# Linear attention of a four-part network: the last head's work in an order of its own, its gate in another PSUM pair

## What is computed

```python
q = silu(causal_dwconv(x @ Wq)); k = silu(causal_dwconv(x @ Wk)); v = x @ Wv
q, k = layernorm(q), layernorm(k)                  # by head
beta = sigmoid(x @ Wb + bb); gate = silu(x @ Wg)
S = (1 - b) * S + b * outer(v_t, k_t)              # by token and head
o_t = S @ q_t
out = (o * gate) @ Wo
```

## Time and profile before

| What | Value |
|---|---|
| Median of 3 runs | 1116.66 us (1115.64 to 1118.02) |
| Profiled execution: own time | 1122.7 us |
| Its span, first to last instruction | 1121.0 us |
| Busy share: TensorE, VectorE, ScalarE, GpSimd | 93%, 70%, 60%, 45% |
| Mean granted TensorE clock | 0.964 of full |
| First gate SiLU and last gating product, start | 480.9 and 821.5 us |
| First ScalarE instruction of the next block | 822.99 us |

### The profile page before, as it was taken

The page is one execution under the profiler, slowest core; times in us unless marked ns, Lnnn a source line. Parts: engine busy times, 40 slices in busy tenths (PEclk is TensorE's granted clock), DMA queues, the critical chain, the costliest instruction groups (busy, mean ns, idle before and its releaser), DMA issues. The chain is left out here.

```text
span 1121.0 us, 18624 instructions
## 1 busy us (share of the span) xinstructions
PE 1043.5 (93%) x6437; PEld 823.9 (74%) x6437; DVE 782.7 (70%) x1785; ACT 677.7 (60%) x1239; POOL 505.4 (45%) x459
## 2 busy tenths in 40 slices
PE   7999999988998998699999999999889999999997
PEld 5433333337786987588998899889779878888997
DVE  5788888717666655699999999998557546333843
ACT  4478778756643454687887787878545444333454
POOL 3251320113039552377676767767604200446534
PEclk9999999969998998699999999999889999999999
DMA  3434333105224300342311221230010122655200
GB/s 90 85 63 62 65 53 56 49 12 169 76 72 136 56 1 6 113 137 65 101 62 52 86 91 52 62 95 25 20 35 12 48 53 59 182 142 169 76 20 20
DMA packets 80633, 79.28 MB, mean 71 GB/s; under 512 B 29320, under 2 KB 67676, under 8 KB 80540
## 3 DMA queue, kind: packets, MB, share of 16 engines
q1 hardware_dynamic: 80228, 77.66, 25.8%
q10 hardware_dynamic: 312, 0.43, 0.3%
HBM read 65.51 MB, written 1.28 MB: 60 GB/s over the span
## 5 line engine op out<-in xcount | busy, mean ns | idle before, releaser
L705 DVE TENSOR_REDUCE attn_row_max<-attn_rows_q 128x1 f32<-128x512 f32 x256 | 159.1, 682 | 29.4 <-PE attn_rows_q L482 29.2
L617 ACT ACTIVATE attn_probs<-attn_rows_k 128x512 f32<-128x512 f32 x256 | 135.4, 600 | 44.0 <-PE attn_rows_k L496 43.7
L496 PE MATMUL attn_rows_k<-attn_q_stack,attn_k_stack 50*128 50x512 f32 x256 | 96.5, 469 | 14.9 <-ACT attn_probs L617 14.8
L482 PE MATMUL attn_rows_q<-attn_k_stack,attn_q_stack 48*128 48x512 f32 x256 | 97.5, 466 | 1.9 <-DMA attn_q_stack<-attn_part 1.2
L2773 DVE TENSOR_TENSOR late_mids<-late_mids,late_bank 128x512 f32<-128x512 f32 (+1 forms) x50 | 34.3, 687 | 78.5 <-PE late_bank L67 75.5
L482 PEld LDWEIGHTS attn_rows_q<-attn_k_stack,attn_q_stack 48*128 48x128 f32 x256 | 42.1, 186 | 55.5 <-DVE attn_row_max L705 43.7
L65 PE MATMUL late_bank<-net_x_part_low,late_w_T 128*128 128x512 f32 (+1 forms) x192 | 77.9, 406 | 0.0
L66 PE MATMUL late_bank<-net_x_part_low,late_w_T 128*128 128x512 f32 (+1 forms) x192 | 76.1, 396 | 0.0
L67 PE MATMUL late_bank<-net_x_part_low,late_w_T 128*128 128x512 f32 (+1 forms) x192 | 76.0, 396 | 0.0
L510 PE MATMUL attn_ctx<-attn_probs,attn_v 128*32 128x512 f32 x512 | 73.7, 652 | 0.0
L496 PEld LDWEIGHTS attn_rows_k<-attn_q_stack,attn_k_stack 50*128 50x128 f32 x256 | 42.2, 191 | 41.9 <-ACT attn_probs L617 36.1
(11 more groups left out here) (407 smaller groups left out, 3415.5 us busy)
## 6 DMA issues: line engine op xcount, KB each, us to landing
lin_mix<-decay_sums SPq DMA_DIRECT2D x16, 512.0 KB, 4.0
lin_q_dec<-decay_sums SPq DMA_DIRECT2D x16, 512.0 KB, 5.4
gold_weight<-gold_weights SPq DMA_DIRECT2D x16, 256.0 KB, 3.5
attn_k_stack<-attn_part SPq DMA_DIRECT2D x30, 128.0 KB, 3.5
s_raw_ring<-in_L_ffn_Wg SPq DMA_DIRECT2D x12, 256.0 KB, 3.1
s_raw_ring<-in_L_ffn_Wu SPq DMA_DIRECT2D x12, 256.0 KB, 3.9
attn_q_stack<-attn_part SPq DMA_DIRECT2D x32, 64.0 KB, 2.3
gold_raw_w_down<-in_L_ffn_Wd SPq DMA_DIRECT2D x1, 2048.0 KB, 12.9
```

Source lines behind the costliest of these rows:

```text
L482: pe.matmul(ps_q[n % 3][:, :], q_stack[rows, h % SLOTS, r * P:(r + 1) * P], k_stack[rows, h % SLOTS, half * HALF:(half + 1) * HALF], start ...
L496: pe.matmul(ps_k[n % 3][:, :], k_stack[rows, h % SLOTS, t * P:(t + 1) * P], q_stack[rows, h % SLOTS, :], start=True, stop=True).then_inc(s ...
L617: act.activation(probs[:, kk % PB, side * HALF:(side + 1) * HALF], ps_k[n % 3][:, :], ACT.Exp)\
L705: dve.tensor_reduce(row_max[:, tile, half:half + 1], ps_q[n % 3][:, :], axis=AX, op=ALU.max)\
```

## The change

Only the last two steps have an order of their own, on four engines. TensorE's loop ends with step 16. Then come, for head 15: turned keys, keys and values, scores, gate, outputs. The gate of head 15 is projected into bank pair 3 instead of pair 0, once the queries are copied out (`q_T_done`); so keys and values no longer wait for its SiLU but for the states of head 14, which read pair 0. ScalarE splits the last gate's weights ahead of the exponentials of head 15. VectorE makes the states of head 15 ahead of its probabilities. GpSimd decays the values of head 15 ahead of its key rows.

```diff
--- before.py
+++ after.py
@@ -1744,8 +1744,8 @@
             if h + 1 < LH:
                 pe.wait_ge(self.v_copied, h + 2)
             else:
-                pe.wait_ge(self.states_done, h)
-            project("gate", pair[0], self.g_projected)
+                pe.wait_ge(self.q_T_done, LH)
+            project("gate", pair[0] if h + 1 < LH else pair[3], self.g_projected)
 
         def project_v(j):
             p, half = divmod(j, 2)
@@ -1774,7 +1774,10 @@
             i.then_inc(self.scored, 1)
 
         def key_values(h):
-            pe.wait_ge(self.g_acted, h + 1)
+            if h + 1 < LH:
+                pe.wait_ge(self.g_acted, h + 1)
+            else:
+                pe.wait_ge(self.states_done, h)
             pe.wait_ge(self.k_rows_done, h + 1)
             pe.wait_ge(self.v_dec_done, h + 1)
             for c in range(NT - 1):
@@ -1806,7 +1809,7 @@
         rows_k(0)
         project_q(1)
         turn_q(0)
-        for n in self.STEPS[2:]:
+        for n in self.STEPS[2:LH + 1]:
             if live(n - 1):
                 rows_q(n - 1)
             turn_k(n - 2)
@@ -1822,6 +1825,11 @@
             if live(n - 1):
                 turn_q(n - 1)
             outputs(n - 2)
+        turn_k(LH - 1)
+        key_values(LH - 1)
+        score(LH - 1)
+        project_gate(LH - 1)
+        outputs(LH - 1)
 
     def high(self, act, m, src, done):
         act.activation(self.parts[m][0][:, :, :], src[:, :, :], ACT.Copy).then_inc(done, 1)
@@ -1886,7 +1894,7 @@
 
         def silu_gate(h):
             act.wait_ge(self.g_projected, h + 1)
-            act.activation(self.gated_out[:, h, :], self.pair[0][:, :], ACT.Silu).then_inc(self.g_acted, 1)
+            act.activation(self.gated_out[:, h, :], self.pair[0 if h + 1 < LH else 3][:, :], ACT.Silu).then_inc(self.g_acted, 1)
 
         def exp_mix(h):
             act.wait_ge(self.masked, h + 1)
@@ -1946,7 +1954,7 @@
         q_transposed(0)
         silu(1, 1, self.k_conved, self.k_acted)
         exp_mix(0)
-        for n in self.STEPS[2:]:
+        for n in self.STEPS[2:LH]:
             if live(n):
                 high_q(n)
             k_transposed(n - 2)
@@ -1972,6 +1980,14 @@
             if live(n):
                 silu(n, 1, self.k_conved, self.k_acted)
                 copy_v(n)
+        k_transposed(LH - 2)
+        silu_gate(LH - 2)
+        high_gate(LH - 1)
+        exp_mix(LH - 1)
+        norm_k(LH - 1)
+        q_transposed(LH - 1)
+        k_transposed(LH - 1)
+        silu_gate(LH - 1)
 
     def dve_first(self, dve):
         dve.wait_ge(self.b_high, 1)
@@ -2094,6 +2110,9 @@
                 variances(n, 0, 3, self.q_rowed, self.q_rstd, self.q_var)
                 variances(n, 1, 2, self.k_rowed, self.k_rstd, self.k_var)
                 norm_q(n)
+        states(LH - 1)
+        probs(LH - 1)
+        gate(LH - 1)
 
     def low(self, pool, m, src, high, done, count):
         pool.wait_ge(high, count)
@@ -2182,6 +2201,12 @@
                 decay_v(n - 1)
             if live(n):
                 power(n, 0, self.q_var, self.q_normed, self.q_rstd)
+        power(LH - 1, 1, self.k_var, self.k_normed, self.k_rstd)
+        decay_q(LH - 2)
+        low("gate", self.wg[(LH - 1) % 2], self.g_high, self.g_split, LH)
+        decay_v(LH - 1)
+        rows_k(LH - 1)
+        decay_q(LH - 1)
 
 
 def golden_and_linear_block(nc, golden, linear, prefetch):
```

## The result

| | Before | Changed |
|---|---|---|
| Median, 20 runs each | 1115.41 us (1112.05 to 1122.43) | 1109.70 us (1105.58 to 1116.88) |
| Profiled execution: own time, span | 1122.7, 1121.0 us | 1112.61, 1110.9 us |
| Mean granted clock of the profile | 0.964 | 0.967 |

The ratio is 0.9944, with a 95% interval of 0.9925 to 0.9963: 0.56% faster, or 4.1 to 8.4 us. The forecast was 5.3 us less than the median of the kernel before; by the medians of these runs it is 5.7.

What follows compares the result with a forecast made beforehand. The last step's chain through TensorE and VectorE to the last gating product, which the next block follows, was taken as the bound. Terms -3.1 - 3.0 + 0.8 = -5.3 us on median 1116.66 gave 1111.4 us; range 1108.5 to 1115.0.

Steps and rivals of the forecast that it cites:

- The pause, -3.1 us: TensorE's 2.96 us idle before head 15's outputs vanishes and a 0.1 us matmul drain overlaps: gain 3.1 us.
- The margins: Last step, TensorE never waits: 0.2 to 0.3 us spare before outputs, 0.3 before scores, 2.6 before keys and values.
- rival of a moved wait: A thin margin breaks and TensorE stands before head 15's scores or outputs, under 1 us: 1111.4 to 1112.4 us; 6%.
- nothing measurable: The last product comes earlier, but something else lets the next block start: 1116 to 1117 us; 4%.
- cover of 2.6 us: GpSimd's key rows for head 15 end at 803.1, 2.6 us before TensorE wants them at 805.7: cost 0.
- The clock, -3.0 us: Without idle time before them, head 15's outputs run at the high clock, 3.55 instead of 6.52 us: gain 3.0 us.
- 0.8 given back: Next block's restart runs low for the mean 4.7 us instead of 3.2: 0.8 us more, bounds -1.6 and +1.5.
- the lucky one: Next block's restart in the profile, low for 3.2 us, the shortest of three low stretches of 3.2 to 6.1 us.
- The rule on pauses: Skill's warning concerns longer pauses, so removing the one before head 15's outputs gives no clock back: sum -3.1 us.
- GpSimd holds VectorE: Moved GpSimd work delays VectorE's head 14 products and states by 7.0 us: 1117.7 us, 1119.2 with longest restart; 3%.

Runs made afterwards that it cites:

- the pause put back: Changed kernel with VectorE repeating head 15's probabilities three times more, so TensorE again idles about 3.2 us before the outputs: median 1115.39 us, ratio 0.9993 to the kernel before.
- the versions with the early gate: Changed kernel with head 15's gate projected ahead of head 14's outputs: ratio 0.9938 to the kernel before; with GpSimd's decayed queries also after the key shift, 0.9951.

## Why the prediction was right

*The pause, -3.1 us.* This term was right. The last step has no idle time of TensorE left, and at equal low time the runs differ by 3.1 us. The margins: probabilities done 0.5 us ahead of the outputs (0.2 to 0.3 counted), key rows 2.7 us ahead (2.6 counted). The rival of a moved wait did not occur, nor did "nothing measurable": the next block's start moved with the product. The experiments show that all of the change is needed for it: undoing VectorE's order costs 1.5 us, the bank 1.4, and the orders of ScalarE and GpSimd 1.0. That last one I had expected at 0 to 0.2 us. It does not touch the forecast's sum, which was for the whole change, but the cover of 2.6 us that the sum counted on is there only with the new GpSimd order.

*The clock, -3.0 us with 0.8 given back.* In the one profile both terms are there: outputs in 3.54 us at 1.00 instead of 6.52, and the next block's restart low for 5.8 us instead of 3.2, which costs (5.8 - 3.2) / 2 = 1.3 us. As a cause it was argued too simply. "Idle for 2.96 us before" was given as the reason of the slow outputs; the pause put back shows 3.3 us of idle time once with the clock up and once with it down. The right statement is about averages: 2.3 us, with a standard error of 0.7, by the low times of these 89 runs. The profiles point the same way: in the three with a pause of 3.0 to 3.3 us before the last outputs these took 6.52, 6.29 and 3.65 us, on average 1.9 us more than 3.54, not 3.0. And the 0.8 us is not borne out. The pause before the next block is 3.27 or 3.28 us in all twelve profiles, and after it TensorE ran low for 0 to 6.1 us (0 in three of them, the changed kernel's second among them), 3.0 us on average; so 3.2 us was an ordinary restart, not the lucky one, and on average nothing is given back there. The outputs' term was about 1 us too large and the restart's 0.8 us too large the other way; the net of 2.2 us beside the measured 2.3 is luck.

*The rule on pauses.* The rule of the Trainium skill, "TensorE: Matmul & The Clock Gate" ("HAM oscillation — how this bites in real kernels") would have left a pause this short out of account. The rows speak against it: 0.53 in the outputs after 2.96 us and 0.56 after 3.28 us, and a gate at 0.61 after a pause of 1.62 us. The low times, 6.3 +- 2.0 us less with the pause of 2.96 us gone, agree with the rows. The other statement of the Trainium skill, on the same page, that the decision is free-running (Part 1), agrees: the same program gave both outcomes.

*GpSimd holds VectorE.* Not so for the moved work: in the changed kernel's trace the 96 state updates took 346 to 350 ns. But the held key shift behind this rival is real: it cost 1.4 us (1.57 instead of 0.17).

*Range and sum.* Predicted ratio 1111.4 / 1116.66 = 0.9953, measured 0.9944. The median of 3 runs that the forecast started from was 1.25 us above the median of 20.

## What to carry to other kernels

At the end of a pipelined loop the steady order is no longer the best: work that nobody waits for (here a gate) belongs behind the work that starts a chain on another engine, and a free bank is what allows it. Where TensorE pauses for some 2 to 3 us, count the pause in full and the clock as an average over executions, not as the one profile shows it; and when a profile is compared with another, compare stretches with the same clock before a cause is read from the spans. A version that moves a pause rather than closing it gains little.

## What the runs showed of the hardware

Whether a pause lowers TensorE's clock differs from execution to execution even at a fixed length: with the pause put back, 3.30 us left it at 1.00 and 3.28 us brought the outputs to 0.56. In the versions with the early gate it was down right after pauses of 1.62 and 2.26 us, and stayed up through one of 2.20 us. The time at the lower level goes with most of the spread of 10 to 15 us between runs of one kernel (correlation 0.9, 0.36 us of time per us at the lower level).

VectorE's key shift, 8 elements per partition, takes 0.17 us free and 1.57 us when a GpSimd instruction on 1024 elements starts before it; it then ends together with that one. The state updates and probability products, which read one input from PSUM, were never held (346 to 351 ns, 1210 to 1225 ns). The Trainium skill, "SBUF — State Buffer" ("Who interferes with whom"), states such a lock for VectorE instructions with two inputs in SBUF against a GpSimd instruction that reads SBUF, and none for those with at most one: rule and rows agree.
